# Two raw buffers and another order of VectorE operations in the compressed interaction layer of a recommendation tower

## The reference

```python
def _cin(x, Ws, bs):                       # x = h = e: [1024, 32, 32]
    for i, (W, b) in enumerate(zip(Ws, bs)):
        z = jnp.einsum('bhd,bmd,ohm->bod', h, x, W.reshape(O, H, F))
        z = jax.nn.relu(z + b[None, :, None])
        ...
            h, direct = (z[:, :half, :], z[:, half:, :])
    out = jnp.concatenate(directs, axis=1)
    return jnp.sum(out, axis=-1)
...
h = jnp.concatenate([z, dense_ctx], axis=1)
h = jnp.maximum(h @ W_top1 + b_top1, 0.0)
h = jnp.maximum(h @ W_top2 + b_top2, 0.0)
y = h @ W_top3
```

## Time and profile before

| | us |
|---|---|
| median of 3 runs | 1181.24 (1178.46 to 1185.1) |
| the profiled execution | 1183.08 |
| its span, first to last instruction | 1181.2 |
| TensorE busy | 1126.7 (95%) |
| VectorE busy | 1082.9 (92%) |
| GpSimd, ScalarE busy | 514.5 (44%), 460.0 (39%) |

### The profile page before, as it was taken

The page is one execution under the profiler, slowest core; times in us unless marked ns, Lnnn a source line. Parts: engine busy times, 40 slices in busy tenths (PEclk is TensorE's granted clock), DMA queues, the critical chain, the costliest instruction groups (busy, mean ns, idle before and its releaser), DMA issues.

```text
span 1181.2 us, 10957 instructions
## 1 busy us (share of the span) xinstructions
PE 1126.7 (95%) x3608; PEld 652.1 (55%) x3608; DVE 1082.9 (92%) x604; ACT 460.0 (39%) x383; POOL 514.5 (44%) x270
## 2 busy tenths in 40 slices
PE   0789999999999999999999999999999999999998
PEld 0345555555555555556555555555556555555554
DVE  1599999999999999999999999999999999999973
ACT  0234444433444433344443334444333444443424
POOL 6604444555444455544445554444555444450000
PEclk9999999999999999999999999999999999999999
DMA  7744443454545344454434455443445544333100
GB/s 222 222 138 133 137 152 121 118 139 137 159 137 142 121 126 136 140 157 138 140 118 130 127 148 148 147 138 120 132 127 148 154 141 142 128 120 112 54 0 1
DMA packets 63413, 154.94 MB, mean 131 GB/s; under 512 B 12753, under 2 KB 29394, under 8 KB 63394
## 3 DMA queue, kind: packets, MB, share of 16 engines
q1 hardware_dynamic: 37202, 96.64, 23.2%
q10 hardware_dynamic: 18000, 53.85, 17.3%
q0 software_dynamic: 8192, 4.21, 3.6%
HBM read 95.79 MB, written 8.39 MB: 88 GB/s over the span
## 4 chain that ended last, share of the span: by engine, by line
DVE 36%; issue 23%; ACT 11%; ACTq 11%; PE 9%; DMA 9%; DVEq 1%; SPq 1%
DVE prod L398 13%; DVE prod_lo L444 12%; DVE raw L437 9%; PE z_ps L530 8%; ACTq L726 5%; ACT prod_hi L753 5%; ACTq L727 5%; DMA x_roll<-x_dram 4%; ACT h_roll L716 4%; DMA x_part<-x_dram 4%; ACT direct L720 1%; DVE raw L420 1%; DVE lo L427 1%; PE mlp_ps L530 1%; SPq L349 1%
## 5 line engine op out<-in xcount | busy, mean ns | idle before, releaser
L530 PE MATMUL z_ps<-prod,w_sb 128*128 128x512 f32 x1536 | 696.5, 600 | 48.1 <-issue 28.4
L303 POOL DMA_INDIRECT gathered<-in_table,rows_sb x256 | 509.9, 1992 | 522.1 <-DVE h2x L451 451.5
L530 PEld LDWEIGHTS z_ps<-prod,w_sb 128*128 128x128 f32 x1536 | 288.5, 191 | 367.2 <-issue 335.0
L753 ACT CAST prod_hi<-raw 128x2048 fp32r<-128x2048 f32 x128 | 244.1, 1907 | 424.4 <-DVE raw L437 365.8
L444 DVE TENSOR_TENSOR prod_lo<-raw,prod_hi 128x2048 fp32r<-128x2048 f32 x128 | 292.3, 2284 | 26.5 <-ACT prod_hi L753 26.5
L437 DVE TENSOR_TENSOR raw<-h_roll,x_roll 128x2048 f32<-128x2048 f32 x128 | 292.7, 2287 | 3.3 <-DMA h_roll<-h_roll 0.9
L398 DVE TENSOR_TENSOR prod<-h_roll,x_roll 128x2048 f32<-128x2048 f32 x128 | 292.5, 2285 | 0.0
L530 PE MATMUL z_ps<-prod_hi,w_hi 128*128 128x512 f32 x520 | 214.9, 493 | 3.0 <-DVE prod_lo L444 3.0
L530 PE MATMUL z_ps<-prod_hi,w_lo 128*128 128x512 f32 x520 | 164.2, 395 | 0.0
L530 PE MATMUL z_ps<-prod_lo,w_hi 128*128 128x512 f32 x520 | 164.1, 395 | 0.0
L398 DVE TENSOR_TENSOR prod<-x_base,x_roll 128x2048 f32<-128x2048 f32 x63 | 143.4, 2287 | 15.1 <-DMA x_roll<-x_dram 8.4
(11 more groups left out here) (56 smaller groups left out, 231.9 us busy)
## 6 DMA issues: line engine op xcount, KB each, us to landing
x_roll<-x_dram SPq DMA_DIRECT2D x128, 512.0 KB
x_base<-x_dram SPq DMA_DIRECT2D x32, 512.0 KB
h_roll<-h_roll ACTq DMA_DIRECT2D x32, 448.0 KB, 3.4
h_roll<-h_roll ACTq DMA_DIRECT2D x32, 384.0 KB
h_roll<-h_roll ACTq DMA_DIRECT2D x32, 320.0 KB
x_dram<-gathered SPq DMA_DIRECT2D x64, 128.0 KB
h_roll<-h_roll ACTq DMA_DIRECT2D x32, 192.0 KB
h_roll<-h_roll ACTq DMA_DIRECT2D x33, 128.0 KB
```

Of the source, the lines that this page charges most:

```text
L303: nc.gpsimd.indirect_dma_start(gathered[:, u, g * DIM:(g + 1) * DIM], None, table, bass.IndirectOffsetOnAxis(ap=rows_sb[:, col:col + 1], a ...
L530: return nc.tensor.matmul(*args, **kw)
L753: nc.scalar.copy(prod_hi[:, b % SPLIT_RING, :, :], raw[:, :, :]).then_inc(hi_ready, 1)
```

## The change

`raw` gets two buffers. The raw product of pair b+1 is made ahead of the remainder of pair b, so that the raw product and its remainder have two operations between them, and the first raw product of a step stands between the two layer-0 products of the next chunk. The second of these and the 16-row product come behind it. `sum_direct` moves from behind whole pair 1 to behind remainder 0. `h2x` moves from behind remainder 1 to behind whole pair 1, ahead of raw pair 2 and remainder 1. ScalarE rounds pair 0 ahead of the 16-row group. TensorE's program is as it was, and so are SyncE's and GpSimd's. In chunk 0 the first raw product follows the first whole pair, as before, and now the 16-row remainder stands behind it.

```diff
+RAW_RING = 2
...
-        raw = sb("raw", [P, PAIR, CHUNK])
+        raw = sb("raw", [P, RAW_RING, PAIR, CHUNK])
...
-                wait(dve, lo_ready, c * PAIRS1 + b)
-                nc.vector.tensor_tensor(raw[:, :, :], h_roll[:, s, PAIR:2 * PAIR, :], twice(x_roll[:, s, b, :]),
+                wait(dve, lo_ready, c * PAIRS1 + b - RAW_RING + 1 if b >= RAW_RING or not_first(c) else 0)
+                nc.vector.tensor_tensor(raw[:, b % RAW_RING, :, :], h_roll[:, s, PAIR:2 * PAIR, :], twice(x_roll[:, s, b, :]),
                                         ALU.mult).then_inc(raw_ready, 1)
...
             def step(c, u, group):
                 s = u % 2
                 if not is_last(c):
-                    products0(c + 1, (u + 1) % UNROLL, group if u < UNROLL - 1 else group + 1)
+                    products0_first(c + 1, (u + 1) % UNROLL)
 
                 dve.wait_ge(h1_ready, 2 * (c + 1))
                 dve.wait_ge(h1_rolled[s][0], (c - s + 2) * 16)
+                if not is_first(c):
+                    split_product(c, u, 0)
+                if not is_last(c):
+                    products0_pair(c + 1, (u + 1) % UNROLL, 1)
+                    product16(c + 1, (u + 1) % UNROLL, group if u < UNROLL - 1 else group + 1)
                 for b in range(ROLLS):
-
-                    split_last = b == 0 and is_first(c)
-                    if not split_last:
-                        split_product(c, u, b)
+                    whole(first1(c) + b, slot1(c) + b, h_roll[:, s, 0:PAIR, :], twice(x_roll[:, s, b, :]))
+                    if b == 0 and is_first(c):
+                        split_product(c, u, 0)
                     if b == 0 and not is_last(c):
                         split_rest16(c + 1)
-                    whole(first1(c) + b, slot1(c) + b, h_roll[:, s, 0:PAIR, :], twice(x_roll[:, s, b, :]))
-                    if split_last:
-                        split_product(c, u, b)
-                    if b == 1 and not_first(c):
-                        sum_direct(c - 1, (u - 1) % UNROLL, group if u else group - 1)
-                    split_rest(c, b)
-
                     if b == 1 and not_first(c):
                         layer2(c - 1, (u - 1) % UNROLL, group if u else group - 1)
+                    if b < ROLLS - 1:
+                        split_product(c, u, b + 1)
+                    split_rest(c, b)
+                    if b == 0 and not_first(c):
+                        sum_direct(c - 1, (u - 1) % UNROLL, group if u else group - 1)
                     if b == 3 and u == 1 and not_first(c, UNROLL):
                         sum_z2(group - 1)
...
             def step(c, u, group):
+                round_products(c, 0)
                 if not is_last(c):
                     round_pairs16(c + 1)
-                round_products(c, 0)
                 if not_first(c):
                     relu1(c - 1, (u - 1) % UNROLL)
                 round_products(c, 1)
```

More of the change, by code:

```diff
@@ L398, in whole, with products0_first @@
                 nc.vector.tensor_tensor(prod[:, slot % RING, :, :], in0, in1, ALU.mult).then_inc(prod_ready, 1)
-            def products0(c, u, group):
+            def products0_first(c, u):
                 s = u % 2
@@ L411, in products0, with products0_pair, product16 @@
                                             ).then_inc(prod_ready, 1)
[L412 to L415, removed]
+                else:
+                    products0_pair(c, u, 0)
+            def products0_pair(c, u, k):
+                s = u % 2
+                for b in range(k * PAIR, (k + 1) * PAIR):
+                    dve.wait_ge(x_roll_loaded[s][b], (c - s + 2) * 8)
+                whole(first0(c) + k, slot0(c) + k, twice(x_base[:, s, :]), x_roll[:, s, k * PAIR:(k + 1) * PAIR, :])
+            def product16(c, u, group):
+                s = u % 2
                 dve.wait_ge(gather_done[u], (group + 1) * (16 * GATHERS))
@@ L443, in split_rest @@
                 slot = b % SPLIT_RING
-                nc.vector.tensor_tensor(prod_lo[:, slot, :, :], raw[:, :, :], prod_hi[:, slot, :, :], ALU.subtract
+                nc.vector.tensor_tensor(prod_lo[:, slot, :, :], raw[:, b % RAW_RING, :, :], prod_hi[:, slot, :, :], ALU.subtract
                                         ).then_inc(lo_ready, 1)
@@ L497, in _ @@
             nc.vector.tensor_copy(w16_sb[:, :, :], w16_raw).then_inc(w16_ready, 1)
-            products0(0, 0, 0)
+            products0_first(0, 0)
+            products0_pair(0, 0, 1)
+            product16(0, 0, 0)
             split_rest16(0)
@@ L752, in round_products @@
                 wait(act, split_used, c * PAIRS1 + b + 1 - SPLIT_RING)
-                nc.scalar.copy(prod_hi[:, b % SPLIT_RING, :, :], raw[:, :, :]).then_inc(hi_ready, 1)
+                nc.scalar.copy(prod_hi[:, b % SPLIT_RING, :, :], raw[:, b % RAW_RING, :, :]).then_inc(hi_ready, 1)
             def round_pairs16(c):
```

## The result

The changed kernel takes **1227.56 us** (median of 4 runs, 1226.52 to 1228.05), the kernel before 1181.93 us in the same comparison (4 runs, 1178.46 to 1185.1). The ratio is 1.0385, with a 95% interval of 1.0355 to 1.0416: slower by 46 us. The forecast was 1227 us. The profiled execution took 1227.14 us, 44.06 more than that of before.

A forecast was written before the change was run, and what follows sets the result against it. TensorE (95% busy), waiting for VectorE (92%), bounds the kernel. Step 33.64 + 0.15 + 1.74 + 0.36 = 35.89 us against 34.43; thirty give +43.8, last step +2.1, total +45.9: 1229.0 profiled, 1227 median; range 1210 to 1258.

The forecast's parts named there:

- What bounds the kernel: Loop steps: TensorE's back-to-back work is 33.64 us of a 34.43 us mean; about 0.65 is waiting for VectorE.
- H: VectorE's 256-column h2x product for the previous chunk; predicted to start 0.20 us after TensorE starts whole pair 1.
- What the change takes away: VectorE's waits for ScalarE's cast, 0.11 behind dependent remainders, 0.3 for an x_roll load: at most 1.3 us per step.
- rival (a): Faster: h2x finds layer 2 done, TensorE runs without waits at 33.79 us a step; about 1160 us; chance 0.09.
- The price of H: h2x ahead of raw pair 2 and remainder 1 closes a loop through both engines: 1.74 and 0.36 us lost per step.
- S1: TensorE's split product needing remainder 1: starts 5.08 us after whole pair 1 starts, lasts 2.90; 1.74 us lost.
- S2: TensorE's split product needing remainder 2: starts 11.68 us after whole pair 1 starts, TensorE ready at 11.01; 0.36 us lost.
- the 19 us that it sets aside: Upper bound if TensorE's split products started from rest cost 3.21 us, not 2.90: up to 19 us more.
- L1 behind R2: On VectorE, remainder 1 behind raw pair 2: a chain of 5.08 us under 3.03 us of TensorE cover.
- The last step: Final loop step, without next-chunk layer-0 products but with the same h2x; TensorE lost nothing there before, so +2.1 us.
- step 0: First step, without h2x: loses cast waits, gains waits for h_roll copies and the 16-row cast; 0, between -2 and +2 us.
- Rival (b): Slower still: TensorE's clock falls in the new gap, 1271 us, or 1235 to 1260 if only sometimes; chance 0.08.

The follow-up runs named there:

- four-gap kernel: Changed kernel with h2x behind remainder 1 and four VectorE operations per step each waiting for the one right ahead: 1164.38 us, again 1163.96 us.
- without gathers: Changed kernel with h2x behind whole pair 2 and GpSimd's gathers replaced by plain SyncE loads: 1164.19 us.
- old start: The four-gap kernel with chunk 0's second layer-0 pair, 16-row product and its cast early, as in the kernel before: 1159.74 us.
- one gap: Changed kernel with h2x behind remainder 1 and only the next chunk's first layer-0 product waiting for remainder 3: 1164.02 us.

## Why the prediction was right, point by point

- **What bounds the kernel**: held. With H out of the loop and the gathers not in the way, the step is packed: TensorE is busy for 96% of the span in the four-gap kernel.
- **What the change takes away**: held. The cast wait of 26.5 us is gone (L452, 0.0), the 0.11 and 0.3 waits too. These parts are worth 1.5% where nothing takes it back (1181.9 to 1164.2 without gathers, 1164.4 and 1164.0 with gaps); rival (a) put this at 1160. One reading is off: for the 16-row remainder the text sets an end of 9.6 us against 7.4, which is its start before (640.75 - 633.40 = 7.35; it ended at 7.77). Nothing hangs on it.
- **The price of H**: each moment of the walk came as put down. Counted from W1's start: H 0.20 (0.20), S1 5.08 (5.08), S1's length 2.90 (2.90), S2 11.68 (11.68), W3 14.58 (14.59). VectorE's stall before H 2.8 us (85.2 / 30 = 2.84; the whole run has 10.5 more in two places, one of 7.6 us as before the change), TensorE's lag at P0 4.9 us (623.28 - 618.41 = 4.87). The step 35.89 (35.92). The moved H alone, in the old order, confirms that it and not the rest of the change costs the time.
- **The range**: what the text lists comes to 6 + 2 = 8 us each way, or up to 27 upward with the 19 us that it sets aside. The 1213 to 1245 (14 and 18 us) is not added up from these terms.
- **The closeness of the number**: partly luck. For the profiled execution the sum gave 1229.0, and it took 1227.14. The medians agree to 0.6 us because the text took off the 1.84 us by which the profiled execution before was above its median; this time it was 0.42 under it.
- **Said too narrowly**: the text names L1 behind R2 as the chain that is paid for. Its own sum had the second part, S2. Bringing L1 forward saved nothing: the cost is that VectorE starts level with TensorE and has five operations to do up to L2.
- **The last step**: the term of +2.1 was mis-sized as a net; it measured +0.4. The loss at H is there. But before, the W behind the 2.67 us wait took 5.37 us at a fallen clock, and after the same wait, 2.66 us, it took 3.67: 1.70 less, and 0.4 + 1.70 is 2.1. The sum carried the fall over without saying so. Both this term and step 0 were put too high, by 1.7 and 1.1 us, and the step's mean too low by 0.03, 0.9 us over 30 steps.
- **Step 0**: 0 within ±2, measured -1.1. That it came so close is luck, since it is the sum of two larger parts that the text did not have: with two raw buffers and the old start step 1 begins at 80.82, 5.1 us ahead of the kernel before, and with the late P1 at 84.82, which takes 4.0 back. TensorE's 16-row products waited for `lo16` until 56.45 us in the changed kernel (4.29 us of idling); with the old start they begin at 51.39.
- **Rival (b)**, the clock falling in the gap of 1.48 us: it did not; the mean granted clock is 0.996.
- **Not seen at all**: that VectorE without pauses would starve GpSimd. The prediction had no term for it. It did not matter here, since no gather of the changed kernel missed its turn for long (3.05 us at most), but rival (a)'s 1160 would have been wrong for the kernel with H simply put behind L1: four of its six executions took 1394 to 1398 us.

**Open:** what decides whether a gather gets its turn at a plain boundary between two VectorE operations. Most do (1.9 to 2.3 us each, one per operation), some miss up to eleven. It is not the moment alone: with one gap, the gathers caught start 1.19 us behind H (609.28 and the H of 608.09), and with H behind L1 and no gap, the first gather of a chunk starts at the same 1.19 us behind H, beside operations at the same distances, and takes 2.25 us (613.89 in the second profiled execution). Both profiled executions of H behind L1 were of the short kind and all four others long, and with H behind W2 the profiled one was the shortest too (1352.53 against 1401 to 1413); whether the profiling plays a part cannot be told from them. That its long ones are the stall shown for H behind W2 is argued from the likeness in time and clock, and from the cure by gaps, not seen in a trace.

## What to carry to other kernels

When an instruction that waits for the other engine is moved in a hand-written order, count from the moment of its release: what must the waiting engine still do until the other one needs it, against what the other one has in hand. If the first sum is larger, it is paid in every step, and no buffer helps. And before packing VectorE with two-input operations from SBUF, look at GpSimd's row of the profile: if its operations run longer beside VectorE than alone, leave one deliberate dependence per step; here it cost nothing that could be measured (1164.0 us with it, 1164.2 without gathers).

## What the runs showed of the hardware

- An indirect load on GpSimd takes 0.94 us with VectorE idle, mostly 1.9 to 2.3 us beside back-to-back operations of 2.20 us, and up to 22.74 us where it keeps missing its turn. It then came through 0.81 to 0.93 us after VectorE paused (0.03 us was enough at 145.30 us with one gap) or began an operation that does not read two inputs from SBUF, in 65 of 65 cases. One pause of 0.32 us per step of 34 us was enough to bring a kernel from mostly 1395 us to 1164 us in each of four executions.
- A VectorE operation that waits for the one right ahead of it starts 2.31 us behind it where others start 2.20 behind the earlier trace rows; P0 with its added wait mostly starts 2.60 us behind the remainder it waits for (617.23 to 619.83); why it is more there was not looked for.
- TensorE's granted clock after a wait of 2.66 to 2.67 us fell in one profiled execution (0.57 over 1122 to 1126 us, kernel before) and not in the other (1.00 over 1164 to 1168 us, changed kernel), at the same place of the program.
